# A macaron layer: running key sums kept in the scores' buffer, the denominators' matmuls in one group, ff_in in one group, and the last tile's key transposition and state update further ahead

## What is computed

```python
# feed-forward part, M = 64, INNER = 16
s = einsum('btd,dm->btm', x, Win) + bin_
h = relu(s[..., None] * W1 + b1)
g = einsum('btmh,mh->btm', h, W2) + b2
out = einsum('btm,md->btd', g, Wout) + bout
# attention, 16 heads of 32 channels; q and k are elu(.) + 1
S = S + k[..., :, None] * v[..., None, :]      # state, per token
z = z + k                                      # running key sum, per token
y = (q @ S) / (sum(q * z) + 1e-6)
x = x + y @ w_proj
```

## Time and profile before

| | before |
|---|---|
| median of 3 runs | 2386.6 us |
| lowest, highest | 2385.26, 2386.83 us |
| profiled execution, first to last instruction (span) | 2384.9 us |
| TensorE matmuls busy | 2291.9 us, 96% |
| VectorE busy | 1936.4 us, 81% |
| ScalarE busy | 1423.0 us, 60% |
| GpSimd busy | 812.4 us, 34% |
| granted TensorE clock, mean | 0.986 |

### The profile page before, as it was taken

The page is one execution under the profiler, slowest core; times in us unless marked ns, Lnnn a source line. Parts: engine busy times, 40 slices in busy tenths (PEclk is TensorE's granted clock), DMA queues, the critical chain, the costliest instruction groups (busy, mean ns, idle before and its releaser), DMA issues.

```text
span 2384.9 us, 74819 instructions
## 1 busy us (share of the span) xinstructions
PE 2291.9 (96%) x32578; PEld 1761.2 (74%) x32578; DVE 1936.4 (81%) x3346; ACT 1423.0 (60%) x2267; POOL 812.4 (34%) x864
## 2 busy tenths in 40 slices
PE   3999999999999999999999999999999999999995
PEld 2777777777777777777777777777777777777774
DVE  6679888888888889888888888888888888887766
ACT  5556566556566556556556557556656556656554
POOL 5223333333333333333333233333233333233222
PEclk7899999999999999999999999999999999999998
DMA  5001111111111111111111101111101111101111
GB/s 173 20 13 45 38 38 56 55 48 45 38 38 55 55 54 39 40 36 56 55 55 37 55 21 56 55 55 37 56 20 56 55 55 37 56 20 38 37 38 37
DMA packets 49657, 111.53 MB, mean 47 GB/s; under 512 B 8241, under 2 KB 10289, under 8 KB 45234
## 3 DMA queue, kind: packets, MB, share of 16 engines
q1 hardware_dynamic: 49330, 106.74, 15.3%
HBM read 72.12 MB, written 34.60 MB: 45 GB/s over the span
## 4 chain that ended last, share of the span: by engine, by line
PE 73%; DVE 16%; issue 5%; POOL 4%; ACT 1%; SPq 1%; DMA 0%; DVEq 0%; POOLq 0%; ACTq 0%
PE bank L1014 33%; PE att L1014 13%; PE att L1043 5%; PE att L1130 5%; PE att L1155 5%; DVE st L681 3%; DVE res L735 3%; DVE acc_psum L719 2%; PE att L1146 2%; PE bank L1118 2%; PE bank L1081 2%; POOL z L370 2%; PE att L1072 2%; DVE yl L698 1%; PE bank L1166 1%
## 5 line engine op out<-in xcount | busy, mean ns | idle before, releaser
L461 ACT ACTIVATE xhat<-res,nmr,rstd 128x512 f32<-128x512 f32 x384 | 302.2, 808 | 354.8 <-DVE nmr L689 292.0
L478 ACT ACTIVATE ffr<-ffs,b1c,w1c 128x512 f32<-128x512 f32 (+2 forms) x544 | 424.4, 805 | 20.0 <-DVE acc_psum L719 13.9
L719 DVE SCALAR_TENSOR_TENSOR acc_psum<-ffr,w2c,acc_psum 128x512 f32<-128x512 f32 (+2 forms) x510 | 379.0, 743 | 48.7 <-ACT ffr L478 27.8
L374 POOL TENSOR_SCALAR_AFFINE_SELECT A<-A 128x512 f32<-128x512 f32 x256 | 157.2, 638 | 704.5 <-ACT A L438 704.5
L362 POOL TENSOR_TENSOR res<-res,hbout 128x512 f32<-128x512 f32 x256 | 352.1, 1393 | 4.0 <-ACT xhat L461 3.4
L681 DVE BATCH_NORM_STATS2 st<-res 128x6 f32<-128x512 f32 x384 | 260.9, 679 | 17.6 <-DMA res<-in_L_attn_x_dram 11.8
L370 POOL TENSOR_TENSOR z<-qT,z 128x512 f32<-128x512 f32 x128 | 165.8, 1295 | 269.8 <-DVE zc L765 119.6
L1014 PE MATMUL att<-xh,wa_h 128*128 128x512 f32 x584 | 235.7, 404 | 1.9 <-DVE xl L698 1.9
L1014 PE MATMUL att<-xl,wa_h 128*128 128x512 f32 x584 | 231.8, 397 | 0.0
L1014 PE MATMUL att<-xh,wa_l 128*128 128x512 f32 x584 | 231.7, 397 | 0.0
L1014 PE MATMUL bank<-wa_h,xh 128*128 128x512 f32 x504 | 214.6, 426 | 0.0
(11 more groups left out here) (142 smaller groups left out, 4969.0 us busy)
## 6 DMA issues: line engine op xcount, KB each, us to landing
xf<-scratch SPq DMA_DIRECT2D x128, 256.0 KB, 4.5
res<-in_L_attn_x_dram SPq DMA_DIRECT2D x31, 1024.0 KB, 5.4
out_dram<-res SPq DMA_DIRECT2D x31, 1024.0 KB, 4.8
scratch<-rden SPq DMA_DIRECT2D x128, 8.0 KB, 1.6
res<-in_L_attn_x_dram SPq DMA_DIRECT2D x4, 256.0 KB, 3.4
kT<-in_L_attn_w_attn_dram SPq DMA_DIRECT2D x1, 1024.0 KB, 5.5
qT<-in_L_attn_w_attn_dram SPq DMA_DIRECT2D x1, 1024.0 KB, 11.9
v<-in_L_attn_w_attn_dram SPq DMA_DIRECT2D x1, 1024.0 KB, 16.3
```

What stands on the lines that cost most here:

```text
L374: eng.affine_select(out=A[:, h, :, :], in_=A[:, h, :, :], compare_op=ALU.is_ge, fill=0.0, base=0, pattern=[[0, 4], [1, P]], channel_multip ...
L461: eng.activation(xhat[t % 2][:, :], res[b % SLOTS][:, t, :], ACT.Identity, bias=nmr[:, n, b % 2, t:t + 1], scale=rstd[:, n, b % 2, t:t + 1 ...
L478: eng.activation(ffr[i % 2][p, w], ffs[p, w], ACT.Relu, bias=b1c[p, i:i + 1], scale=w1c[p, i:i + 1]).then_inc(s_hr, 1)
L719: eng.scalar_tensor_tensor(psum[p, w], r[p, w], w2c[p, i:i + 1], psum[p, w], ALU.mult, ALU.add).then_inc(s_hm, 1)
```

## The change

The running key sums move from `z2` to `A` (under the name `z`), with room for all four groups. The scan waits for `s_num` (the last `attend` of the block before) instead of `s_den`. The staging of Wout and bout that `z2` also held goes to `ktok`, of which there are now two, and the copy into one waits only for the update before the last (`s_up`). On TensorE the four `den` stand together behind `values(j, 0, 1)`, and both parts of `ff_in` behind them. `key(j, 3)` stands ahead of `channels(j + 1, 1)` on TensorE and ahead of `score(j, 3, 0)` on ScalarE; `update(j, 3)` stands right behind `attend(j, 3)` on TensorE, and on VectorE behind `ynorm(j, 3)`. The order in which `give` hands out banks follows.

```diff
-        ktok = sb("ktok", [P, C])
+        ktok = [sb(f"ktok{i}", [P, C]) for i in range(2)]
-        z2 = sb("z2", [P, 2, BLK])
...
-            give(ATT + RING, ("k", j, 0), ("k", j, 1), ("q", j, 0), ("q", j, 1), ("k", j, 2), ("k", j, 3), ("q", j, 2),
-                 ("den", j, 0), ("q", j, 3), ("v", j, 0), ("key", j, 0))
+            give(ATT + RING, ("k", j, 0), ("k", j, 1), ("q", j, 0), ("q", j, 1), ("k", j, 2), ("k", j, 3), ("q", j, 2), ("q", j, 3), ("v", j, 0), ("key", j, 0), ("den", j, 0))
...
-            give(RING, ("y", j, 1), ("up", j, 2), ("xT", j + 1, 1))
+            give(RING, ("y", j, 1), ("up", j, 2), ("key", j, 3), ("xT", j + 1, 1))
             give_all("sc", j, 3)
             give(RING, ("y", j, 2))
-            give(ATT + RING, ("xT", j + 1, 2), ("xT", j + 1, 3), ("y", j, 3), ("o0", j - 1, 0), ("o1", j + 2, 0),
-                 ("key", j, 3), ("up", j, 3), ("o0", j - 1, 1), ("o1", j + 2, 1), ("o0", j - 1, 2), ("o1", j + 2, 2),
-                 ("o0", j - 1, 3), ("o1", j + 2, 3))
+            give(ATT + RING, ("up", j, 3), ("xT", j + 1, 2), ("xT", j + 1, 3), ("y", j, 3), ("o0", j - 1, 0), ("o1", j + 2, 0), ("o0", j - 1, 1), ("o1", j + 2, 1), ("o0", j - 1, 2), ("o1", j + 2, 2), ("o0", j - 1, 3), ("o1", j + 2, 3))
...
+        z = wp_st
+        wo_st, bout_st = ktok[0], ktok[1]
...
@@ GpSimd, zsum @@
-                z = z2[:, g % 2, :]
-                eng.tensor_tensor(z, qT[:, g, :], z, ALU.mult).then_inc(s_zq, 1)
+                eng.tensor_tensor(z[:, g, :], qT[:, g, :], z[:, g, :], ALU.mult).then_inc(s_zq, 1)
@@ ScalarE, key @@
-                e.wait_ge(s_up, nth_update(b, t) - 1)
-                copy(ktok[:, :], bank[spot["key", b, t][0]][:, :], s_ktok)
+                e.wait_ge(s_up, nth_update(b, t) - 2)
+                e.wait_ge(s_wol, 1)
+                copy(ktok[nth_update(b, t) % 2][:, :], bank[spot["key", b, t][0]][:, :], s_ktok)
@@ ScalarE, loop: key(j, 3) from ahead of normalise(L3, j, 0) to ahead of score(j, 3, 0) @@
@@ VectorE, zsum @@
-                e.wait_ge(s_den, 4 * b + g - 1)
-                e.wait_ge(s_mbout, 1)
-                e.wait_ge(s_wol, 1)
+                e.wait_ge(s_num, 4 * b)
+                e.wait_ge(s_walo, 4)
@@ VectorE, loop: update(j, 3) from behind outer(j, 3) to behind ynorm(j, 3) @@
@@ TensorE, loop @@
                     project(j, 0, 2)
-                    den(j, 0)
-                    den(j, 1)
                     project(j, 0, 3)
                     values(j, 0, 0)
                     key(j, 0)
                     values(j, 0, 1)
+                    den(j, 0)
+                    den(j, 1)
                     den(j, 2)
                     den(j, 3)
                 if on(j - 1) or on(j + 2):
                     ff_in(j, 0)
+                    ff_in(j, 1)
                 if on(j):
                     values(j, 1, 0)
-                if on(j - 1) or on(j + 2):
-                    ff_in(j, 1)
-                if on(j):
                     values(j, 1, 1)
...
                     update(j, 2)
                     outer(j, 1, 1)
+                if on(j) and updates(j, 3):
+                    key(j, 3)
                 if on(j + 1):
                     channels(j + 1, 1)
                 if on(j):
                     scores(j, 3)
                     outer(j, 2, 0)
                     attend(j, 3)
+                if on(j) and updates(j, 3):
+                    update(j, 3)
...
                 if on(j - 1) or on(j + 2):
                     ff_out(j, 0)
-                if on(j) and updates(j, 3):
-                    key(j, 3)
                 if on(j):
                     outer(j, 3, 1)
-                if on(j) and updates(j, 3):
-                    update(j, 3)
```

More of the change, by code:

```diff
@@ L277, in _ @@
             load(1)
-            eng.dma_start(z2[0:1, 1, :], bout.rearrange("(a n) -> a n", a=1)).then_inc(s_bout, 16)
+            eng.dma_start(bout_st[0:1, :], bout.rearrange("(a n) -> a n", a=1)).then_inc(s_bout, 16)
             for h in range(4):
@@ L290, in _ @@
             for h in range(2):
-                eng.dma_start(z2[M * h:M * h + M, 0, :], Wout).then_inc(s_wo, 16)
+                eng.dma_start(wo_st[M * h:M * h + M, :], Wout).then_inc(s_wo, 16)
             for n in (0, 2):
@@ L354, in wout_lo @@
                 e.wait_ge(s_woh, 1)
-                eng.tensor_tensor(wo_l[:, :], z2[:, 0, :], f32(wo_h[:, :]), ALU.subtract).then_inc(s_wol, 1)
+                eng.tensor_tensor(wo_l[:, :], wo_st[:, :], f32(wo_h[:, :]), ALU.subtract).then_inc(s_wol, 1)
             def bias(half, b, t):
@@ L547, in _ @@
             e.wait_ge(s_wo, 32)
-            copy(wo_h[:, :], z2[:, 0, :], s_woh)
+            copy(wo_h[:, :], wo_st[:, :], s_woh)
             e.wait_ge(s_wa[0], 16)
@@ L753, in zsum @@
                 e.wait_ge(s_elu[1], 4 * b + g + 1)
-                e.wait_ge(s_den, 4 * b + g - 1)
-                e.wait_ge(s_mbout, 1)
-                e.wait_ge(s_wol, 1)
+                e.wait_ge(s_num, 4 * b)
+                e.wait_ge(s_walo, 4)
                 if not first:
                     e.wait_ge(s_zc, carried(b - 1, g))
-                eng.tensor_tensor_scan(z2[:, g % 2, :], kT[:, g, :], kT[:, g, :], 0.0 if first else zc[:, g:g + 1],
+                eng.tensor_tensor_scan(z[:, g, :], kT[:, g, :], kT[:, g, :], 0.0 if first else zc[:, g:g + 1],
                                        ALU.add, ALU.bypass).then_inc(s_scan, 1)
@@ L764, in carry @@
                 e.wait_ge(s_scan, 4 * b + g + 1)
-                eng.tensor_copy(zc[:, g:g + 1], z2[:, g % 2, BLK - 1:BLK]).then_inc(s_zc, 1)
+                eng.tensor_copy(zc[:, g:g + 1], z[:, g, BLK - 1:BLK]).then_inc(s_zc, 1)
             def rec(b):
@@ L1097, in den @@
                 for t in range(TILES):
-                    op = eng.matmul(o[D * t:D * t + D, 0:P], heads_of[:, g, :], z2[:, g % 2, t * P:t * P + P],
+                    op = eng.matmul(o[D * t:D * t + D, 0:P], heads_of[:, g, :], z[:, g, t * P:t * P + P],
                                     start=g == 0, stop=g == 3)
@@ L1165, in update @@
                         d, n = slice(D * h, D * h + D), slice(g * P + D * h, g * P + D * h + D)
-                        op = eng.matmul(o[d, g * D:g * D + D], ktok[:, n], v[:, t, n], start=True, stop=True)
+                        op = eng.matmul(o[d, g * D:g * D + D], ktok[nth_update(b, t) % 2][:, n], v[:, t, n], start=True, stop=True)
                 op.then_inc(s_up, 1)
@@ L1181, in _ @@
             o = take("bout", 0, 0)
-            eng.matmul(o[:, :], tri[0:1, :], z2[0:1, 1, :], start=True, stop=True).then_inc(s_mbout, 1)
+            eng.matmul(o[:, :], tri[0:1, :], bout_st[0:1, :], start=True, stop=True).then_inc(s_mbout, 1)
             for n in range(2):
```

## The result

The changed kernel takes 2393.56 us (8 runs, 2391.13 to 2394.42), the kernel before 2387.08 us beside it (8 runs). The ratio is 1.0025, with an interval of 1.0016 to 1.0035: slower by a quarter of a per cent, where 2355 us was forecast. The profiled execution spans 2391.2 us at a granted clock of 0.987 (0.986 before), so the clock did not change.

What follows compares the result with a forecast made beforehand. TensorE, working through its program almost without a pause, was taken as the bound. Savings of 0.88 us per odd and 1.09 per even block, times 16, took 31.5 from 2384.9, giving 2355 us, range 2349 to 2362.

Steps and rivals of the forecast that it cites:

- den together: The four den groups in one run on TensorE: 0.50 us saved per odd block, 1.54 per even block.
- rival 1: VectorE's addition comes sooner and hides channels' bank wait: 10.9 us less, 2344 us; chance 0.07.
- rival 2: The wait for GpSimd's product comes back in even blocks, about 1.0 us each: 2371 us; chance 0.08.
- rival 3: Joining groups makes no switch and no run cheaper: 23.4 us missing, 2378 us; chance 0.08.
- rival 4: VectorE hands back banks later than TensorE wants them, so blocks keep their pitch: 2387 us; chance 0.03.
- ff_in: Both parts in one run, 256 matmuls in 3.85 us: 0.17 us saved, plus 0.21 for a switch pair.
- rival 5: Clock falls at the new wait at the even block's end: slower, 2423 us if five us run low; chance 0.04.
- The last tile's key: Moved ahead of channels(j + 1, 1): scores 1.09 us later, less 0.41, so 0.68 us lost per even block.
- The last tile's update: Even block's end: 0.39 us on TensorE in either place, but channels(j + 1, 3) waits for ysplit; 0.15 us lost.
- The sum: Odd block 0.88 us saved, even block 1.09, pair 1.97; times 16 is 31.5 us, leaving a 2353.4 us span.

Runs made afterwards that it cites:

- Experiment 8: The kernel before, with only the denominators' bank changed to one of the ring in every block: 2380.54 us, ratio 0.9981.
- e6: The kernel of experiment 1 with key(j, 3) behind scores(j, 3), its copy behind the scores' copies, denominators in the ring: 2394.92 us, ratio 1.0037.
- e3: Also written experiment 3: the changed kernel with 64 small matmuls added at TensorE's very start: 2399.2 us, ratio 1.0054.
- e4: The kernel before with only the last tile's key and update moved, and their bank order: 2411.18 us, ratio 1.0098.
- experiment 9: The kernel before with only the denominators changed, in one group and a ring bank; ff_in apart, key and update unmoved: 2351.39 us, ratio 0.9856.
- experiment 10: Two runs: e6, then e6 with channels(j + 1, 2) given a bank of the ring: 2351.11 us, ratio 0.9857.
- (4): The changed kernel with three of the six matmuls of values(j, 1, 0) put between the parts of ff_in: 2379.11 us, ratio 0.9974.
- experiment 1: The changed kernel with the first part of values(j, 1) back between the two parts of ff_in: 2371.49 us, ratio 0.9933.
- experiment 7: The same run as e4: the kernel before with only the last tile's key and update moved, and their bank order: 2411.18 us, ratio 1.0098.

## Why the prediction was wrong, step by step

- **"den together": right.** The group took 1.01 us where 1.00 was taken, with no wait worth naming. Alone, it brought 2385.46 - 2351.39 = 34.1 us for 32.6 worked out. Experiment 8 shows that about 5 us of it are the bank and not the joining. Rivals 1 to 4 are out: the wait for `s_x2` is not hidden, the wait for the product did not return, joining `den` does make it cheaper, and without pauses the blocks do get shorter.
- **"ff_in": this step failed.** It priced 256 matmuls in one run by the pitch of 128, 3.85 us for the run, which takes for granted that instructions reach TensorE as fast as it works through them, and took the joining as a gain of 0.17 and, with the switch pair, 0.38 a block. The run took 5.42 us in the block shown, and the joining cost 22.1 us in place of the 12 it should have brought. It put the lower bound of the joining at nothing, and had no case in which joining loses. None of the rivals had one either: rival 3, no gain from joining, ended at 2378, and only rival 5, the clock, went the other way. The clock stayed at 1.00 in the changed kernel from 71.5 to 2361.9 us, behind the new wait of 0.45 us and its transposes too. Where it did fall inside the blocks, TensorE had stood still for longer just before: 1.97 us in nine places of e6 and 1.7 in a tenth, 1.6 and 1.7 us in two of e3, 1.9 us in one of e4. Such a stop does not always lower it: seven of the sixteen waits in e6 left it at 1.00.
- **"The last tile's key": the forecast held for this order.** 1.05 us measured for 1.09, and 7.3 us of new wait; with the update, 14.4 us for 13.3 (experiment 9). That it need not cost anything is what experiment 10 adds: one group further on, with its banks in the ring, both moves are free, though they gain nothing either (2351.11 against 2351.39).
- **"The last tile's update": right.** `update` takes 0.42 us there, and the `outer` ahead of `channels(j + 1, 3)` 1.63 (849.09 to 850.72) where 1.48 without a wait was its length before: 0.15.
- **The sum** with the measured pauses: a span of 2353.4, plus the 31.6 of the 29 pauses, plus 29 x 0.25 for the new starts, is 2392.3; 2391.2 was measured.

What the runs show of the pause's cause: it stands at a border between packets and moves with it (experiment 3), it shrinks with the number of wide matmuls ahead of it (4), and in the traces of the changed kernel and of e3 it ends 1.2 to 1.6 us after a packet of instructions has landed, 1.36 in the block shown. What is derived from them, and not shown apart: that TensorE works one packet ahead and no further. It fits in numbers, those of the block shown first. From the place where the sequencer, some 33 small matmuls ahead of the array, goes over the first border (about when the run starts, 741.05) to the first matmul of the packet behind the second (744.90) it is 3.8 us, made up of 1.1 until the request, 1.35 for the transfer and 1.36 until it is used. The matmuls from 33 before a border to the next border are 161, 2.3 us at 0.0143, so 1.5 us are missing; 1.32 + 0.25 stand there. With six wide matmuls in place of six of them it is 155 x 0.0143 + 1.6 = 3.8 us, just enough, which would be why the kernel before and experiment 1 have no such pauses. That block is one of the slower ones. The median of the 29 is 2.44 us from request to use, 3.55 with the 1.1: then 1.25 us are missing in a joined run (the median pause is 1.03, and 0.25 comes to it), 0.35 with three wide matmuls between (158 x 0.0143 + 0.9; 0.26 measured), and none with six. Where the sequencer stands was inferred from these times; no row has it.

The Trainium skill ("Runtime: NRT & Kernel Launch", Instruction fetch mechanics) says that each engine refills its instruction memory in blocks of 16 KiB, 256 instructions, ahead of use, which the packets here agree with, and that the cost of a border is mostly hidden by the time it takes to issue instructions. This trace differs on the second point: a run of weight loads and matmuls 0.0143 us apart is not slow enough to hide it.

## What to carry to other kernels

Before joining groups of many small instructions, count how many instructions are then issued without a long one between, and hold their time against what the profile shows between an instruction packet's request and its use; a few wide matmuls in the middle are worth more than the switch they cost. When idle time has no releaser and sits inside a run of identical instructions, look at the instruction queue, and shift the whole program by some instructions: if the pause moves with the border between packets, it is the supply. (Take another number than half a packet, as here, since 64 matmuls forward and 64 back then look alike.) And after each edit of an order by which buffers are handed out, read which buffer every product got: twice here (experiments 7 and 10) a product landed in a bank with a late reader, for 8 and 44 us, the second time because the wait pulled the clock down with it.

## What was unexpected of the hardware

- TensorE pauses for 0.74 to 1.59 us (up to 1.75 in experiment 3) inside a run of 256 matmuls on 32 x 64 pieces, at the border of a 16 KB packet, although the packet holds only instructions that are fully known ahead. From a packet's request to the use of what is in it 2.2 to 2.9 us pass.
- A run that goes on after such a pause costs about 0.25 us besides it.
- Moving a program by 128 instructions alone changed its time by 5.8 us down in one kernel (2371.49 to 2365.71) and 5.6 up in another (2393.56 to 2399.2), and by nothing in the kernel before (0.9996).
- Behind nine of e6's sixteen waits of about 2 us the granted clock fell from 1.00 to 0.50; with a tenth such stretch that is some 16 us by estimate, besides the 32.1 of the waits; waits of 0.45 us at nearly the same place did not.
